# Flamingo-style two-layer network, second self-attention: matmuls of ones over each unit's own block, in place of GpSimd's sum of two blocks

## What is computed

```
q = einsum('bsc,hcd->bhsd', xn, wq)
k = einsum('btc,hcd->bhtd', yn, wk)
v = einsum('btc,hcd->bhtd', yn, wv)
a = softmax(einsum('bhsd,bhtd->bhst', q, k) * D ** -0.5, axis=-1)
if causal:
    a = a * (arange(t)[None, :] > arange(s)[:, None])
o = einsum('bhst,bhtd->bhsd', a, v)
```

## Time and profile before

| | |
|---|---|
| three runs | 1650.4, 1652.21, 1652.48 us |
| profiled execution | 1654.29 us, of which the span from first to last instruction is 1652.5 |
| mean granted TensorE clock over the span | 0.922 of full speed |
| busy over the span: TensorE, VectorE, GpSimd, ScalarE | 1350.0, 935.6, 737.4, 708.6 us |
| part d on the trace's clock | first scores shortly before 605, last output product at 1001.47 |
| part d, steady slots (slot 8 to slot 125) | 621.30 to 970.91 |

### The profile page before, as it was taken

The page is one execution under the profiler, slowest core; times in us unless marked ns, Lnnn a source line. Parts: engine busy times, 40 slices in busy tenths (PEclk is TensorE's granted clock), DMA queues, the critical chain, the costliest instruction groups (busy, mean ns, idle before and its releaser), DMA issues. The chain is left out here.

```text
span 1652.5 us, 56201 instructions
## 1 busy us (share of the span) xinstructions
PE 1350.0 (82%) x22797; PEld 855.1 (52%) x22798; DVE 935.6 (57%) x2365; ACT 708.6 (43%) x1493; POOL 737.4 (45%) x1263
## 2 busy tenths in 40 slices
PE   4899999999977959999999986969888969705860
PEld 2555555555545725555555554645554537605860
DVE  3466666666634656777777754456566556611431
ACT  1455555555534426556656652414333324302430
POOL 3233333333322837787787774842222125351016
PEclk9999999999997979999999997979989879856995
DMA  4340000000000310000000001210101013201114
GB/s 103 104 128 16 20 16 19 17 19 13 13 12 26 96 51 12 22 22 12 22 22 19 9 12 58 79 48 21 29 26 29 21 56 111 63 37 47 55 59 135
DMA packets 129455, 69.42 MB, mean 42 GB/s; under 512 B 20312, under 2 KB 125356, under 8 KB 129212
## 3 DMA queue, kind: packets, MB, share of 16 engines
q1 hardware_dynamic: 127164, 61.75, 13.3%
q0 software_dynamic: 2048, 4.20, 0.8%
HBM read 41.80 MB, written 24.12 MB: 40 GB/s over the span
## 5 line engine op out<-in xcount | busy, mean ns | idle before, releaser
L595 ACT ACTIVATE space<-scores 128x512 f32<-128x512 f32 x576 | 314.1, 551 | 344.8 <-PE scores L454 258.2
L681 DVE TENSOR_REDUCE space<-scores 128x2 f32<-128x512 f32 (+1 forms) x512 | 308.7, 624 | 223.2 <-PE scores L454 150.9
L823 POOL TENSOR_SCALAR_AFFINE_SELECT space<-space 128x512 f32<-128x512 f32 x128 | 81.6, 637 | 290.0 <-ACT space L595 290.0
L425 PE MATMUL scores<-space 32*128 32x256 f32 (+1 forms) x2304 | 196.8, 411 | 16.3 <-DVE space L681 10.5
L835 POOL TENSOR_TENSOR space<-space 128x1024 f32<-128x1024 f32 x64 | 151.5, 2368 | 0.0
L454 PE MATMUL scores<-space 32*128 32x256 f32 (+1 forms) x2048 | 149.7, 357 | 0.0
L425 PEld LDWEIGHTS scores<-space 32*128 32x128 f32 x2304 | 94.7, 188 | 99.8 <-DVE space L681 75.5
L827 POOL TENSOR_SCALAR_AFFINE_SELECT space<-space 128x512 f32<-128x512 f32 x128 | 87.9, 687 | 71.6 <-ACT space L595 71.5
L401 PE MATMUL misc<-w_a_li_w,space 128*32 128x128 f32 x2048 | 74.7, 290 | 34.1 <-ACT space L1113 15.1
L454 PEld LDWEIGHTS scores<-space 32*128 32x128 f32 x2048 | 84.0, 187 | 16.7
L1084 ACT ACTIVATE space<-scores 128x512 f32<-128x512 f32 x64 | 37.9, 597 | 113.7 <-PE scores L994 90.0
(11 more groups left out here) (309 smaller groups left out, 2855.5 us busy)
## 6 DMA issues: line engine op xcount, KB each, us to landing
space<-in_x SPq DMA_DIRECT2D x32, 128.0 KB, 2.2
x<-space SPq DMA_DIRECT2D x16, 256.0 KB, 2.9
space<-xx SPq DMA_DIRECT2D x32, 128.0 KB, 2.1
xo<-space SPq DMA_DIRECT2D x32, 128.0 KB
space<-xo SPq DMA_DIRECT2D x16, 256.0 KB
space<-xm SPq DMA_DIRECT2D x32, 128.0 KB, 2.2
space<-x SPq DMA_DIRECT2D x16, 256.0 KB, 3.7
sorted_in<-zeros SPq DMA_DIRECT2D x10, 256.0 KB
```

Of the source, the lines that this page charges most:

```text
L425: last = pe.matmul(a.score_bank(j)[:, 0:n], q[rows, e * P:(e + 1) * P], keys[rows, 0:n], start=not cut, stop=True, skip_group_check=True)
L595: act.activation(pt[:, 2 * pair:2 * pair + 2, lo:S], a.score_banks(pair)[:, :, S + lo:2 * S], ACT.Exp, bias=0.0, scale=1.0)\
L681: last = dve.tensor_reduce(out[:, c % 2, 2 * pair:2 * pair + 2], banks[:, :, 0:n], AX.X, ALU.max, negate=True)
L823: pool.affine_select(out=block, in_=block, compare_op=ALU.is_ge, fill=0.0, base=0, pattern=[[0, 4], [1, P]], channel_multiplier=-1).then_i ...
```

## The change

GpSimd's `add` is gone with its signal and the waits for it. The value step multiplies the ones with the unit's own block `pt` in both halves, right behind the value matmuls, so a quad has two groups where it had one. The accumulation starts with (c=0, e=0) and stops with (c=3, e=1). The wait for the denominators saved before moves with the first group from e=1 to e=0. The tile `both` stays allocated.

```diff
@@ SelfAttention.__init__
-        if mask == "after":
-            each.update(summed=QUADS)
@@ tensor_self, values(n)
-            if e == 1:
-                if c == 0:
-                    wait(pe, s["den_saved"], b)
-                wait(pe, s["summed"], QUADS * b + c + 1)
-                for j in range(4):
-                    last = pe.matmul(strip(k.turned[0], j)[:, b % 2 * S:(b % 2 + 1) * S], k.ones_column[:, c], k.both[:, c % 2, j],
-                                     start=(c == 0), stop=(c == 3), skip_group_check=True)
+            if c == 0 and e == 0:
+                wait(pe, s["den_saved"], b)
+            for j in range(4):
+                last = pe.matmul(strip(k.turned[0], j)[:, b % 2 * S:(b % 2 + 1) * S], k.ones_column[:, c], pt[:, j, :],
+                                 start=(c == 0 and e == 0), stop=(c == 3 and e == 1), skip_group_check=True)
         last.then_inc(s["pv_done"].sem, 1)
@@ scalar_self, exps(i, t)
-        if a.mask == "after":
-            wait(act, s["summed"], (t - TURNED) // 2 + 1)
@@ gpsimd_self
-    def add(t):
-
-        b, c, e = a.unit(t)
-        wait(pool, s["exped"], 2 * (t + 1))
-        wait(pool, s["pv_done"], t - 3)
-        pool.tensor_tensor(k.both[:, c % 2], k.pt[:, (t - 1) % TURNED], k.pt[:, t % TURNED], ALU.add).then_inc(s["summed"].sem, 1)
-
@@ the loop over slots in gpsimd_self
             mask(i - a.lag)
-            if a.mask == "after" and (i - a.lag) % 2 == 1:
-                add(i - a.lag)
```

## The result

The changed kernel takes 1667.26 us (median of 4 runs, 1664.47 to 1668.83), the one before 1651.31 in the same comparison (4 runs, 1650.07 to 1652.48). The ratio is 1.0095, with a 95% interval of 1.0077 to 1.0112: slower by about 16 us. The forecast was 1667.1.

A forecast was written before the change was run, and what follows sets the result against it. TensorE's matmul order was taken to bound the stage, with VectorE narrowly pacing even slots. Terms 18.3 - 0.9 - 2.5 = +14.9 us on 1654.29 gave 1669.2 profiled, 1667.1 as median; range 1661 to 1675.

The forecast's parts named there:

- Ones in even slots: Slots 8 to 124, every second one: 59 added groups of 0.43 us, less 0.12 room each, cost +18.3 us.
- A: Rival for even slots: VectorE's maxima hide the added ones, slots stay 2.75 us, median 1648.8; chance 0.05.
- B: Rival for even slots: no room at all, each of 59 pays 0.43 us, median 1674.2; chance 0.12.
- D: Rival on the added groups: their weight loads do not hide, +0.88 us in each of 59, 1719; chance 0.01.
- Waits of TensorE: Odd slots lose the add wait, 45 times 0.03 us; the moved denominator wait costs 0.5; together -0.9 us.
- 0.55 where the next step starts with a wait that is already fulfilled: Group of ones to the next step: 0.55 us with a fulfilled wait, against 0.43 to the next group.
- room of 0.12 us: Even slots: 0.66 us from last group to next window, where a 256-column group needs 0.54 to 0.55.
- Run-out: Draining end of the stage: without GpSimd's adds on the path, the last ones begin 2.5 us sooner, -2.5 us.
- the split: Run-out: GpSimd's splitting of the last maxima no longer queues behind an add, so their transposing comes 0.91 us earlier.
- Slot 5: Its chain over VectorE's maxima and L755 sets its length, so it keeps 3.90 us though the split comes sooner.
- Rival C: Odd slots shrink too: slot 5 loses up to 0.3 us in 16 batches, 4.8 us less, 1662.3; chance 0.09.

The follow-up runs named there:

- e3: Changed kernel with the ones of every even slot issued twice; ratio 1.0289 to the kernel before, median 1695.8 us.
- e4: Changed kernel with the even slots' ones over 128 queries instead of 256; ratio 1.0044 to the kernel before, median 1659 us.
- e5: Changed kernel with one more, already fulfilled wait ahead of every group of ones; ratio 1.0092 to the kernel before, median 1667.3 us.
- e1: Changed kernel with GpSimd's 64 adds put back, their result unused, only ScalarE's refill waiting for them; ratio 1.0100 to the kernel before.
- e6: Kernel before, with adds dropped and ones over each unit's own block for the last ten units only; ratio 1.0016 to the kernel before.
- e9: Kernel before, with own blocks and no adds for the last ten units, and slot 5's output piece first; ratio 1.0001 to the kernel before.

## Why the prediction was right, and where a step was not

- **Ones in even slots (+18.3).** Right, by its own steps: 0.54 instead of 0.66 ahead of the window, 3.06 us in each of the 59 slots, a batch of 25.00 instead of 23.77, +18.30 in the steady part; slot 126 stayed at 2.75. e3 and e4 show the room itself: 0.43 for a second group, 0.095 for one of 0.21. Rivals A and B fall with them. D falls with the 0.43 of the added group, whose eight loads hid as the others do. D's price was misread as well: the loads overlap one another, and rows 8 give 15.1 us of busy time for 64 groups, 0.24 for each and not 0.88. Loads that don't hide would then cost 14 us, and the forecast would be about 1681.
- **Waits of TensorE (-0.9).** Wrong. The step that sets 0.24 us from L509 to L516 against 0.21 from L509 to the next group of an even slot put the difference down to the wait. Odd slots kept their length without the wait, and e5 added 128 waits at no cost. The 0.24 belongs to the distance between the first and the second group behind the scores: L502 to L507 in an even slot is 0.24 as well (799.90 to 800.14), whichever lines these are. The term measures 0. The "0.55 where the next step starts with a wait that is already fulfilled" fails in the same way: the value piece at 796.84 starts with such a wait too (`side`), 0.43 behind the ones. The room of 0.12 us did not rest on this reason, since it was read from distances.
- **Run-out (-2.5).** Right in place and nearly in size. The last ones moved by 2.47 us (21.67 to 19.20); the split alone is 0.89 by e1 (9.92 against 9.03), estimated 0.91. A further 0.42 came behind them: the last but one output piece took 1.08 us instead of 1.40 and the last one 1.86 instead of 1.94, as the clock fell later. That was in no step, and e6 shows that it can go the other way.
- **Slot 5.** Right: 3.91 before and after. Rival C falls.
- **The sum.** 18.3 - 2.9 is 15.4, against 14.9 predicted. The wait term took off 0.9 that is not there, and the run-out gave 0.4 more than forecast; the two leave the half microsecond. The medians differ by 15.95, which the parts' 15.4 meets within the measurement. That the forecast of 1667.1 came within 0.2 us of 1667.26 is luck: it started from 1652.21, and the kernel before took 1651.31 in the comparison, 0.9 less, while the difference came out 1.05 more.

The list of waits would have misled: it names VectorE as what the weight loads waited for, 59.7 us before and 54.1 after, although VectorE paced the 59 even slots before and none of them after. The list of the changed kernel (625 to 1010 us) and the loads of its even slot at 801.77, put down to maxima that had ended 0.41 earlier:

```profile
PEld scores L423 <- DVE space L675: 54.1, 104, 1.2
```
```profile
801.77 0.31 PEld L423 LDWEIGHTS scores<-space 32*128 32x128 f32 x8 [0.41 <-DVE space L675]
```

## What to carry to other kernels

Where a kernel walks one list of slots on all engines, cost an edit slot by slot: the distance from the last group's start to the next window, against the shortest distance that the same kind of group shows elsewhere in the trace, is the room, and only what exceeds it is paid, in every slot. Taking 151 us of work off an engine that nobody waits for gave under 3 us, all at the end where the pipeline drains, while 27.5 us of matmuls (64 groups of 0.43) given to an engine with next to no idle time cost 18.3. A gain of 0.2 to 0.4% in a part can be read exactly in the slots and still not show in the time of the whole, so say which of the two was shown.

## What the runs showed of the hardware that was not expected

- A fulfilled wait ahead of a group of ones cost TensorE no time: with one more ahead of each of 128 groups, 118 of them in slots 8 to 125, the steady part changed from 367.91 to 367.92 us (e5).
- In these timelines a step from one form of tile to another takes 0.11 us more than one within a form. A group of 256 columns in strips of 32 output columns takes 0.43 to a group of the same form, and 0.54 or 0.55 to scores (32 rows by 128) or to a full transpose (128 by 128). The Trainium skill ("TensorEngine Tiling (Array Packing)", Key Properties) says that changing the tiling mode drains TensorE; these 0.11 us fit that. They don't show it: no run tested the change of form apart from the work around it, and from L423 to L448 inside a window, where the form stays and the type goes from float32 to bf16, it is 0.54 too (801.77 to 802.31).
- The same run-out can meet either clock. Behind the last ones TensorE waits 3.57 or 3.58 us for VectorE in the changed kernel, in the one before, in e6 and in e9; the output piece after it took 1.08, 1.40, 1.93 and 1.18 us, with the granted clock at full speed (2.4 GHz) in the first and at half in e6. e6 and e9 have the same run-out. Each was profiled once, and what makes the clock fall sooner in one than in another was not tried.
- Whole executions differed by more than the smaller gains, along with their clock: in the last comparison the kernel before took 1646.15 us at a mean granted clock of 0.924 and 1664.05 at 0.916, and over its 23 runs the time rose by 7 us for each 0.01 that the clock was lower. The relation is loose (correlation -0.62). In the steady part of d the clock was 1.00 in the profile of every kernel here, so what differs seems to lie outside it.
